# Cross-attention and ternary feed-forward: the probabilities of both tiles in five blocks of 128 keys, with new instruction orders

## The reference

```python
# layernorm(x), then attention over the 77 context rows: 16 query heads in 4 groups, 4 key heads of 32
qh = rope(layernorm(x) @ Wq); kh = rope(ctx @ Wk); vh = ctx @ Wv
scores = einsum('bghsd,bhad->bhsa', qh, kh)          # summed over the 4 groups g
attn = softmax(scores / HEAD_DIM ** 0.5, axis=-1)    # over 77 keys a
out = einsum('bhsa,bhad->bhsd', attn, vh).mean(axis=1) @ Wo
x = x + out
# feed-forward: ternary weights, input quantised to 8 bits by one scale for all of x
x = x + quantised_matmul(layernorm(x), sign(w) * (abs(w) > 0.5 * mean(abs(w)))) * scales + bias
```

## Time and profile before

| what | us |
|---|---|
| median of 3 runs | 1150.74 (1150.21 to 1151.82) |
| the profiled execution's own time | 1148.87 |
| its span, first to last instruction | 1147.1 |
| TensorE matmul busy | 1096.0 (96%) |
| VectorE busy | 1018.8 (89%) |
| ScalarE busy | 988.1 (86%) |
| GpSimd busy | 738.6 (64%), all of it before 835 us |
| mean granted TensorE clock | 0.980 of full speed |

### The profile page before, as it was taken

How to read it: one execution, slowest core, us unless ns; L and a number is a source line. 1 busy time by engine, 2 the same in 40 slices (tenths; PEclk the granted TensorE clock), 3 DMA queues, 4 the chain that set the end, 5 groups by cost and what they waited for, 6 DMA issues and landing times.

```text
span 1147.1 us, 45345 instructions
## 1 busy us (share of the span) xinstructions
PE 1096.0 (96%) x14519; PEld 894.0 (78%) x14519; DVE 1018.8 (89%) x1836; ACT 988.1 (86%) x2403; POOL 738.6 (64%) x1547
## 2 busy tenths in 40 slices
PE   7998999999999999999999999999689999999991
PEld 6997999999999999999999999999545555555550
DVE  4653799999999999999999999999889999999991
ACT  4565899999999999999999999999789999999990
POOL 4675999999999999999999999999700000000000
PEclk9999999999999999999999999999889999999996
DMA  8774365665656565665656543332029999999996
GB/s 297 217 200 132 92 218 179 203 190 193 208 188 207 177 206 181 199 200 187 212 179 208 178 147 100 98 100 79 3 111 388 423 422 427 425 418 389 401 414 281
DMA packets 97241, 260.28 MB, mean 227 GB/s; under 512 B 42537, under 2 KB 53993, under 8 KB 76722
## 3 DMA queue, kind: packets, MB, share of 16 engines
q1 hardware_dynamic: 97154, 259.75, 64.9%
q10 hardware_dynamic: 48, 0.07, 0.0%
HBM read 137.11 MB, written 122.64 MB: 226 GB/s over the span
## 4 chain that ended last, share of the span: by engine, by line
POOL 44%; PE 34%; issue 15%; DVE 2%; POOLq 1%; ACT 1%; DMA 0%; SPq 0%; DVEq 0%; ACTq 0%
PE sc_ps L1317 10%; PE pT_ps L1317 10%; POOL qr_sb L589 8%; POOL rs_sb L581 7%; POOL pw_sb L596 6%; POOL qa_sb L561 6%; PE y_ps L1112 5%; POOL pw_sb L603 5%; POOL os_sb L608 3%; POOL o_sb L610 3%; POOL ve_sb L574 2%; POOL mean L616 2%; PE xT_ps L1101 1%; PE y_ps L1300 1%; POOL os_sb L614 1%
## 5 line engine op out<-in xcount | busy, mean ns | idle before, releaser
L1257 PEld LDWEIGHTS xT_ps<-wqs,xT_sb 128*128 128x128 f32 x2048 | 239.5, 192 | 48.8 <-ACT xT_sb L723 48.8
L1257 PE MATMUL xT_ps<-wqs,xT_sb 128*128 128x128 f32 x2048 | 264.0, 282 | 2.9 <-ACT xT_sb L723 2.9
L1273 PE MATMUL pT_ps<-v_blk,pT_sb 128*128 128x68 f32 x1536 | 186.7, 271 | 0.4 <-ACT pT_sb L735 0.4
L1273 PEld LDWEIGHTS pT_ps<-v_blk,pT_sb 128*128 128x128 f32 x1536 | 182.2, 192 | 1.9 <-ACT pT_sb L735 1.2
L745 ACT ACTIVATE e_sb<-e_sb,rs_sb 128x308 f32<-128x308 f32 x256 | 127.4, 545 | 62.9 <-DVE e_sb L956 62.9
L973 DVE SCALAR_TENSOR_TENSOR x_sb<-x_sb,mv_sb,y_ps 128x512 f32 (+1 forms) x256 | 177.9, 736 | 2.7 <-PE y_ps L1249 2.7
L788 ACT ACTIVATE x_sb<-x_sb,mean 128x512 f32 (+1 forms) x256 | 168.7, 707 | 0.0
L686 ACT ACTIVATE sq_sb<-x_sb 128x512 bf16 (+1 forms) x256 | 162.6, 635 | 1.1 <-DVE x_sb L973 0.8
L980 DVE TENSOR_REDUCE amax<-x_sb (+1 forms) x128 | 155.1, 1212 | 0.0
L943 DVE TENSOR_REDUCE mx_sb<-sc_ps 128x8 f32<-128x616 f32 x128 | 102.4, 800 | 46.0 <-PE sc_ps L1238 46.0
L723 ACT ACTIVATE xT_sb<-xT_ps 128x512 f32<-128x512 f32 x256 | 139.2, 597 | 2.8 <-PE xT_ps L1179 2.7
(11 more groups left out here) (140 smaller groups left out, 2253.0 us busy)
## 6 DMA issues: line engine op xcount, KB each, us to landing
out_y<-x_sb SPq DMA_DIRECT2D x112, 1024.0 KB, 10.5
x_sb<-in_x SPq DMA_DIRECT2D x128, 512.0 KB, 3.8
x_sb<-out_y SPq DMA_DIRECT2D x48, 1024.0 KB, 15.3
x_sb<-in_ctx SPq DMA_DIRECT2D x38, 256.0 KB, 3.9
k_blk<-k_scr SPq DMA_DIRECT2D x256, 9.6 KB, 1.7
v_scr<-x_sb SPq DMA_DIRECT2D x38, 68.0 KB, 2.9
k_scr<-x_sb SPq DMA_DIRECT2D x38, 64.0 KB, 3.0
v_blk<-v_scr SPq DMA_DIRECT2D x128, 10.2 KB
```

What stands on the lines that cost most here:

```text
L1257: last = pe.matmul(bank[0][:, t * HD:(t + 1) * HD], xT_sb[:, t, c, :], wqs[:, c, :], start=c == 0, stop=c == EC - 1)
L1273: last = pe.matmul(bank[6][:, at0:at0 + 2 * VC], pT_sb[:, t, c * P:(c + 1) * P], v_blk[:, slot, c, c:c + 2, :].rearrange("p h d -> p (h d) ...
```

## The change

The probabilities of both tiles of a pair are treated as one row of 616 keys, cut in 5 blocks of 128 (starts 0, 128, 256, 384, 488). A block can reach from tile 0 into tile 1; it holds keys of 2 or 3 (tile, head) pairs, and its matmul writes all of their columns at once: 5 value matmuls of 3, 3, 2, 3, 3 x 34 columns in place of 6 of 2 x 34. `v_blk` now holds the values of a batch twice, once for each tile's place. ScalarE copies `xT_sb` and `pT_sb` with one instruction each, and both squares stand before the exponentials. GpSimd runs `pw_sb` before `qr_sb`, `o_sb` before the high part, and the mean before the low part. VectorE's `bn_stats` of tile 1 moves from the end of a step to behind the reciprocal of the next one. The diff, without the renamed semaphores and blank lines:

```diff
@@ -46,9 +46,10 @@
 HALF = P // 2
-CHUNKS = 3
-CR = -(-SC // CHUNKS)
-STARTS = [min(c * CR, SC - P) for c in range(CHUNKS)]
+CHUNKS = 5
+STARTS = [min(c * P, 2 * SC - P) for c in range(CHUNKS)]
+FIRST_HEAD, HEADS_OF = (0, 1, 3, 4, 5), (3, 3, 2, 3, 3)
@@ -91,11 +92,11 @@
 for c, start in enumerate(STARTS):
-    for h in range(HEADS):
-        lo, hi = max(c * CR, CTX * h), min(c * CR + CR, SC, CTX * (h + 1))
+    for n in range(2 * HEADS):
+        lo, hi = max(c * P, CTX * n), min(c * P + P, CTX * (n + 1))
         if lo < hi:
-            assert c <= h <= c + 1
-            out.append((c, lo - start, hi - lo, h, lo - CTX * h))
+            assert FIRST_HEAD[c] <= n < FIRST_HEAD[c] + HEADS_OF[c]
+            out.append((c, lo - start, hi - lo, n - FIRST_HEAD[c], n % HEADS, lo - CTX * n))
 return out
@@ -137,7 +138,7 @@
 e_sb = sb("e_sb", [P, 2, 2, SC])
-pT_sb = sb("pT_sb", [P, 2, CHUNKS * P])
+pT_sb = sb("pT_sb", [P, CHUNKS, P])
 pv_sb = sb("pv_sb", [P, 2, HEADS, VC])
@@ -146,7 +147,7 @@
 k_blk = sb("k_blk", [P, 2, SC])
-v_blk = sb("v_blk", [P, 2, CHUNKS, HEADS, VC])
+v_blk = sb("v_blk", [P, 2, CHUNKS, max(HEADS_OF), VC])
 bn_sb = sb("bn_sb", [P, 2, 2, 6])
...
@@ -373,8 +374,8 @@
-for c, r, n, h, a in segs:
-    sp.dma_start(v_blk[r:r + n, k % 2, c, h, :], v_scr[bass.ds(b * CTX + a, n), h, :])\
+for c, r, n, m, h, a in segs:
+    sp.dma_start(v_blk[r:r + n, k % 2, c, m, :], v_scr[bass.ds(b * CTX + a, n), h, :])\
       .then_inc(v_in[k % 2], 16)
@@ -426,7 +427,7 @@
 elif first < j <= first + 3:
-    v_step(b, b, SEGS[(j - first - 1) * 2:(j - first) * 2])
+    v_step(b, b, SEGS[(j - first - 1) * 4:(j - first) * 4])
@@ -549,24 +550,25 @@
 proj, rope, score, value, head, resid, stat, rstd = (stage(i, k, g, lag) for lag in range(RSTD + 1))
+js, ks = i - SCORE, (k - SCORE) % UN
+at = slice(0 if score else 1, 2 if rstd else 1)
+both = score or rstd
+def turned(table, dst):
+    half = slice(2 * (rope[1] % 2), 2 * (rope[1] % 2) + 2)
+    pool.tensor_tensor(dst[:, :].rearrange("p (t h d) -> p t h d", t=2, h=HEADS),
+                       q_sb[:, :].rearrange("p (t h d) -> p t h d", t=2, h=HEADS),
+                       table[:, half, :].unsqueeze(2).broadcast_to([P, 2, HEADS, D]),
+                       ALU.mult).then_inc(rope_mul, 1)
 if rope:
...
     pool.wait_ge(q_copied, j + 1)
-    half = slice(2 * (kj % 2), 2 * (kj % 2) + 2)
-    def turned(table, dst):
-        pool.tensor_tensor(dst[:, :].rearrange("p (t h d) -> p t h d", t=2, h=HEADS),
-                           q_sb[:, :].rearrange("p (t h d) -> p t h d", t=2, h=HEADS),
-                           table[:, half, :].unsqueeze(2).broadcast_to([P, 2, HEADS, D]),
-                           ALU.mult).then_inc(rope_mul, 1)
     turned(qcos, qa_sb)
-if score or rstd:
-    at = slice(0 if score else 1, 2 if rstd else 1)
-    js, ks = i - SCORE, (k - SCORE) % UN
+if both:
     if score:
@@ -575,11 +577,19 @@
     turned(qsin, qb_sb)
-if score or rstd:
+if both:
...
                        ve_sb[:, k % 2, :, at], mhalf[:, :, at], ALU.pow).then_inc(rs_ready, 1)
+if head:
+    j, kj, gj = head
+    pool.wait_ge(rinv_ready, j + 1)
+    pool.tensor_tensor(pw_sb[:, :, :, :].rearrange("p t h d -> p (t h) d"),
+                       pv_sb[:, :, :, 0:D + 1].rearrange("p t h d -> p (t h) d"),
+                       rinv_sb[:, :, :].rearrange("p t h -> p (t h)").unsqueeze(2)
+                       .broadcast_to([P, 2 * HEADS, D + 1]), ALU.mult).then_inc(o_part, 1)
 if rope:
@@ -590,14 +600,6 @@
 if head:
-    j, kj, gj = head
-    pool.wait_ge(rinv_ready, j + 1)
-    pool.tensor_tensor(pw_sb[:, :, :, :].rearrange("p t h d -> p (t h) d"),
-                       pv_sb[:, :, :, 0:D + 1].rearrange("p t h d -> p (t h) d"),
-                       rinv_sb[:, :, :].rearrange("p t h -> p (t h)").unsqueeze(2)
-                       .broadcast_to([P, 2 * HEADS, D + 1]), ALU.mult).then_inc(o_part, 1)
-if head:
     j, kj, gj = head
@@ -605,16 +607,17 @@
 pool.wait_ge(o_part, 2 * j + 2)
+pool.tensor_tensor(o_sb[:, :, :], pw2_sb[:, :, 0, :], pw2_sb[:, :, 1, :],
+                   ALU.add).then_inc(o_ready, 1)
 pool.tensor_tensor(os_sb[:, :, 0, :], pw2_sb[:, :, 0, 0:D], pw2_sb[:, :, 1, 0:D],
                    ALU.add).then_inc(o_ready, 1)
-pool.tensor_tensor(o_sb[:, :, :], pw2_sb[:, :, 0, :], pw2_sb[:, :, 1, :],
-                   ALU.add).then_inc(o_ready, 1)
+pool.wait_ge(o_ready, 2 * j + 1)
+pool.tensor_tensor(mean1[:, bass.ds(2 * j, 2)], o_sb[:, :, D], mv_sb[:, kj, :, 0],
+                   ALU.add).then_inc(mean_ready, 1)
 pool.wait_ge(o_ready, 2 * j + 2)
...
                    ALU.subtract).then_inc(os_ready, 1)
-pool.tensor_tensor(mean1[:, bass.ds(2 * j, 2)], o_sb[:, :, D], mv_sb[:, kj, :, 0],
-                   ALU.add).then_inc(mean_ready, 1)
@@ -719,23 +722,23 @@
     at_least(act, q_done, j)
-    for t in range(2):
-        act.activation(xT_sb[:, t, :, :].rearrange("p c (h r) -> p c h r", h=2),
-                       rows_of(xT_ps, t * E // 2, EC), ACT.Copy).then_inc(xT_copied_t, 1)
+    act.activation(xT_sb[:, :, :, :].rearrange("p t c (h r) -> p (t c) h r", h=2),
+                   rows_of(xT_ps, 0, 2 * EC), ACT.Copy).then_inc(xT_copied, 1)
     if isinstance(j, int) and j == 0:
         keys_out(CT, CLAST)
+if stat:
+    square(0)
 if value:
...
     at_least(act, pv_done, j)
-    for t in range(2):
-        act.activation(pT_sb[:, t, :].rearrange("p (c h r) -> p c h r", c=CHUNKS, h=2),
-                       rows_of(pT_ps, t * CHUNKS * HALF, CHUNKS), ACT.Copy).then_inc(pT_copied_t, 1)
+    act.activation(pT_sb[:, :, :].rearrange("p c (h r) -> p c h r", h=2),
+                   rows_of(pT_ps, 0, CHUNKS), ACT.Copy).then_inc(pT_copied, 1)
 if stat:
-    square(0)
+    square(1)
 if score:
@@ -751,8 +754,6 @@
     act.activation(q_sb[:, :], bank[0][:, 0:2 * HD], ACT.Copy).then_inc(q_copied, 1)
-if stat:
-    square(1)
@@ -931,6 +932,10 @@
     dve.reciprocal(rinv_sb[:, :, :], pv_sb[:, :, :, D + 1]).then_inc(rinv_ready, 1)
+if rope:
+    j, kj, gj = rope
+    dve.bn_stats(bn_sb[:, kj % 2, 1, :], x_sb[:, kj // 2, 2 * (kj % 2) + 1, :]).then_inc(bn_step, 1)
 if score:
@@ -980,10 +985,6 @@
                       apply_absolute_value=True).then_inc(amax_done, 1)
-if proj:
-    j, kj, gj = proj
-    dve.bn_stats(bn_sb[:, kj % 2, 1, :], x_sb[:, kj // 2, 2 * (kj % 2) + 1, :]).then_inc(bn_step, 1)
@@ -1218,9 +1219,9 @@
 held(exp_done_t, 2 * j + 2, exp_count, 2)
-for t in range(2):
-    for c, start in enumerate(STARTS):
-        last = halves(pT_ps, (t * CHUNKS + c) * HALF, e_sb[:, kj % 2, t, start:start + P])
+both = e_sb[:, kj % 2, :, :].rearrange("p t s -> p (t s)")
+for c, start in enumerate(STARTS):
+    last = halves(pT_ps, c * HALF, both[:, start:start + P])
 last.then_inc(pT_done, 1)
...
@@ -1264,15 +1265,14 @@
             pe.wait_ge(v_in[slot], gj * (2 * V_DMAS * 16) + (kj // 4 + 1) * (V_DMAS * 16))
-        pe.wait_ge(pT_copied_t, 2 * j + 2)
-        for t in range(2):
-            for c in (0, 2, 1):
-                at0 = (t * HEADS + c) * VC
-                last = pe.matmul(bank[6][:, at0:at0 + 2 * VC], pT_sb[:, t, c * P:(c + 1) * P],
-                                 v_blk[:, slot, c, c:c + 2, :].rearrange("p h d -> p (h d)"),
-                                 start=c == 0, stop=c == 1)
+        pe.wait_ge(pT_copied, j + 1)
+        for c in (0, 2, 4, 1, 3):
+            at0, n = FIRST_HEAD[c] * VC, HEADS_OF[c]
+            last = pe.matmul(bank[6][:, at0:at0 + n * VC], pT_sb[:, c, :],
+                             v_blk[:, slot, c, 0:n, :].rearrange("p h d -> p (h d)"),
+                             start=c == 0, stop=c == 3)
         last.then_inc(pv_done, 1)
 steps(pe, step)
```

More of the change, by code:

```diff
@@ L265, in build @@
         rs_ready = sem("rs_ready")
-        xT_done, xT_copied_t, q_done, q_copied = (
-            sem(n) for n in ("xT_done", "xT_copied_t", "q_done", "q_copied"))
+        xT_done, xT_copied, q_done, q_copied = (
+            sem(n) for n in ("xT_done", "xT_copied", "q_done", "q_copied"))
         rope_mul, qr_ready, qT_done, qT_copied = (
@@ L271, in build @@
             sem(n) for n in ("sc_done", "mx_ready", "sub_done", "exp_done_t"))
-        pT_done, pT_copied_t, pv_done, pv_copied = (
-            sem(n) for n in ("pT_done", "pT_copied_t", "pv_done", "pv_copied"))
+        pT_done, pT_copied, pv_done, pv_copied = (
+            sem(n) for n in ("pT_done", "pT_copied", "pv_done", "pv_copied"))
         rinv_ready, o_part, o_ready, os_ready, wq_mean, wq_centred = (
@@ L1253, in step @@
                     j, kj, gj = proj
-                    pe.wait_ge(xT_copied_t, 2 * j + 2)
+                    pe.wait_ge(xT_copied, j + 1)
                     for t in range(2):
```

## The result

The changed kernel takes 1133.91 us (median of 4 runs, 1128.25 to 1138.45) against 1150.47 for the kernel before beside it: a ratio of 0.9855 (95% interval 0.9809 to 0.9901). A second comparison gave 1134.54 against 1150.64, 0.9861 (0.9835 to 0.9887). It is faster by 1.4%; the forecast was 1197 us and slower.

What follows compares the result with a forecast made beforehand. TensorE bounds the kernel before; SyncE's queue would bound the changed one. Issues +31.6, holds +28.8, absorbed -8.0 and remaining steps -5.8 make +46.6 us on 1148.87: 1195.5, as a median 1197 us, range 1148 to 1242.

Steps and rivals of the forecast that it cites:

- SyncE becomes the bound: SyncE's DMA queue, batches 4 to 51: slack gone, 11.8 us a batch before added holds, against 10.82 for the compute engines.
- The compute engines' 5.41 us a step: Four compute engines: a step falls from 5.59 to 5.41 us, 0.18 less, with VectorE as their bound.
- The gap before the maximum: VectorE: the moved bn_stats directly before the maximum makes it wait, adding 0.04 us a step.
- The price of six more issues, 2.88 us: SyncE's queue: 12 v pieces instead of 6, each added issue at 0.48 us, 2.88 us more a batch.
- s = 0.6: SyncE's queue: change in time of held issues per batch, taken as +0.6 us, bounds -2.5 and 2.2.
- the two rate terms: SyncE's loop: +28.7 us for 47 batches at 11.8 instead of 11.19, and +28.8 for 48 x 0.6 of holds.
- the tail: The 32 steps after SyncE's loop: run at the compute engines' pace, 0.18 us less each, -5.8 us.
- the 8.0 us of v slack: Between the last v piece's landing and its first reader: delay absorbed there, -8.0 us in the sum.
- the 2.9 of the last batch: End of SyncE's loop: the last batch's own six added issues, +2.9 us in the sum.
- Break-even: SyncE's period at which loss and gain cancel within 0.2%: 11.4 us a batch, chance 0.09.
- the first rival: SyncE does not bind: holds shrink 0.4 us a batch for break-even, 1.0 to clear it; 1129 us, chance 0.16.

Runs made afterwards that it cites:

- e1: The changed kernel with 4 of each batch's 12 v pieces left out, so part of the value product is missing: 1123.74 us, ratio 0.9767.
- g1: The changed kernel with the loop's x1 stores issued by ScalarE instead of SyncE: 1125.96 us, ratio 0.9788.
- g2: g1 with VectorE's bn_stats of tile 1 back at the end of the step: 1123.81 us, ratio 0.9770.
- h1: The changed kernel with the 12 v pieces issued ahead of the x1 store in SyncE's loop: 1124.87 us, ratio 0.9772.
- i1: g2 without the last of four feature chunks in tile 0's q projection, so its q is incomplete: 1115.98 us, ratio 0.9697.
- e3: The changed kernel with the old orders on GpSimd, ScalarE and VectorE; five blocks, 12 v pieces and single copies stay: 1147.73 us, ratio 0.9969.
- g3: The kernel before with the x1 stores issued by ScalarE: 1153.29 us, ratio 1.0023.
- f1: The kernel before with each of its 6 v pieces cut in two, 12 issues for the same rows: 1168.66 us, ratio 1.0145.
- f2: The kernel before with each of its 6 v pieces brought twice, the second time to an unread spare tile: 1155.72 us, ratio 1.0050.

## Why the prediction was wrong, point by point

**SyncE becomes the bound: right.** Its wait for x1 fell from 91.1 us to 1.1 and e1 gave it back. TensorE waits for x, as was named as one of two possibilities, not for `v_blk`.

**The compute engines' 5.41 us a step: right in size, by luck, and wrong in the engine.** 5.40 in the tail and in e1, g1, g2, h1. It is TensorE's bound (i1). Two errors met: TensorE was to take 5.27 and takes 5.40; VectorE was to take 5.41, and in its old order it runs 5.35 (i1). TensorE's matmul records had been priced by their weight loads alone. The value matmuls' weight loads fell by 12 x 0.118 - 10 x 0.120 = 0.22 us (forecast 0.24) and the transposes by 0.06 (0.08). All loads together went from 460.05 us at 5.594 a step to 454.70 at 5.397 (g1): 5.15 to 4.91 us, -0.24. The rest of TensorE's step, in which no load ran, grew from 0.45 to 0.49 us. The single copies took 1.026 and 0.697 us (1.02 and 0.70 forecast). The gap before the maximum was right: in g1 the maximum has 4.1 us of idle time in 83, 1.2 of them a wait for the scores, so 0.035 us each. GpSimd had three waits on itself; with the one before `pw2_sb` in the earlier trace rows, the other two were:

```profile
L608 POOL TENSOR_TENSOR os_sb<-pw_sb 128x64 fp32r<-128x64 f32 x80 | 24.0, 300 | 10.2
...
L614 POOL TENSOR_TENSOR os_sb<-o_sb,os_sb 128x64 fp32r<-128x64 f32 x80 | 25.3, 317 | 6.3
```

Of these 6.4, 10.2 and 6.3 us the first and the last are gone, as forecast, 0.16 us a step; the middle one stays and stands before `o_sb` now (10.5). e3 shows that the new orders were needed to get below 5.56.

**The price of six more issues, 2.88 us, with s = 0.6 us of hold on top: this step failed.** From the first v piece to the first k piece it was 4.89 us a batch and is 6.97 (means of 47 batches): +2.08, where 3.48 was forecast. The forecast took the hold for a length that comes on top of the issues. It ends at a point of time: 4.35 us behind the second x load's issue before (mean; the one batch of the earlier trace rows has 4.26), 4.90 now, +0.55, with x loads that land at 5.7 us instead of 4.1. That later end is what s = 0.6 foresaw, but it is no term of its own, as more issues fit before it. Up to the first issue behind the hold it is 3.35 us before and 3.89 now, and in it stand mostly five of the twelve pieces (27 of 47 batches; four in 12) instead of three of six. So about seven, not nine, are paid behind it: 2 x 0.48 = 1.0 us less. And these seven cost 0.44 us each, not 0.48 to 0.51, as some of them find their address ready: 0.4 us less.

The control runs give the same in the prediction's two terms. Without holds the six pieces take 3.07 us from the start of the first to the start of the issue behind them (g3, mean; 3.02 in the batch shown), the twelve 5.44 (h1, mean; 514.42 - 509.05 = 5.37 in the batch above):

```profile
502.80 2.74 SPq L377 DMA_DIRECT2D v_blk<-v_scr  x6
505.82 1.82 SPq L371 DMA_DIRECT2D k_blk<-k_scr  x4
```

That makes 2.37 us for six more issues, 0.40 each, where 2.88 was forecast. The time in holds is then 4.89 - 3.07 = 1.82 us a batch before and 6.97 - 5.44 = 1.53 now: s was -0.3, not +0.6. The rest of a batch's queue stayed at 4.0 us. The need is 8.91 + 2.08 = 11.0, and 11.00 was measured.

**The sum, made again with what was measured.** The loop starts 0.7 us earlier; 47 x (11.03 - 11.19) = -7.5 in place of the +57.5 that the two rate terms gave together; the tail 32 x (5.40 - 5.60) = -6.4 (forecast -5.8); together -14.6, and -14.8 were measured. So neither the 8.0 us of v slack nor the 2.9 of the last batch appear. The slack was read off the wrong transfer: TensorE stopped for x, whose loads fall behind with the queue from the first batches on (four waits from 140 to 200 us, up to 1.4 us each), and no wait for a v piece appears at all. With the 4.3 us lost in the second part, which lies within what that part varies by, it is -10.3, measured -10.6.

**Break-even** was put at 11.4 us a batch, with the v slack in it; it lies at the period of before, 11.19: f1's 47 x (11.54 - 11.19) = +16.5 stands against a last maximum that starts 15.4 us later (831.6) and 17.8 us by the medians. An error of 13% in the need, 12.4 for 11.0, decided the sign, as what counts is its distance from 11.2, times 47. In the prediction's unit the outcome is 11.0 - 11.8 = -0.8 us a batch, between the 0.4 and the 1.0 of the first rival, which had a chance of 0.16. That rival was right that the time in holds shrinks, by 0.3 us, and the cheaper issues gave the rest; it was wrong that SyncE then does not bind.

**The Trainium skill's sentence** (DMA: Bandwidth & Descriptors, section Issuing engines are not separate DMA queues) that the time to initiate a DMA "is usually small relative to the DMA itself" holds here of each DMA alone: a k piece's issue takes 0.32 us and it lands after 1.7. It does not follow that issues cost nothing, and the prediction was right not to go by that: 4 fewer give 10 us (e1), and 6 more cost 18 (f1). That section's subject, which sequencer issues, is what g1 used.

**What stays open** is what an issue waits for when it is held. With the store in SyncE's queue right behind the x loads, the hold stands at the second to fifth v piece; in g1, h1 and i1, where it does not stand there, shorter holds appear at the eleventh to sixteenth issue behind the x loads; in g3, with 10 small issues and no store, there is hardly any. A limit on what is in flight would fit all of it, but no run measured one.

## What to carry to other kernels

When an in-order queue that issues DMAs runs near its slack, don't price added issues one by one on top of its stalls: find the instant at which a stall ends, count how many issues fit before it and pay only for those behind. When a forecast rests on the difference of two nearly equal periods, the sign is settled by an error of a few per cent, so the chance must be split near even however clear the bound is. And when a queue is the bound, first look for the order of its own entries: small transfers that others wait for belong ahead of a large store that nobody waits for (1134 to 1125 us here for an exchange of two lines).

## What the runs showed of the hardware that was not expected

- With the 1 MB store in front of them, small DMA issues of SyncE are held, two a batch in the kernel before and two to four in the changed one, until 4.35 and 4.90 us on average behind the second x load's issue; without it in front, the first nine pieces take 0.23 to 0.35 us each (g1; so do all six in g3, but for one issue in 47 batches), and the holds come later or hardly at all.
- An issue with an address computed in registers starts 0.18 to 0.2 us after its forerunner's end, 0.09 if the address is already there (f2, alternating). Over 12 issues that and the hold make 0.32 us a batch (11.54 against 11.22).
- The x loads land later when both are issued close together with the store right behind: median 5.7 us in the changed kernel and f1 (loads 0.7 us apart), 4.8 in e1 (1.9 apart), 4.1 in the kernel before (2.9 apart). Without the store behind them it is 4.0 in g1 (1.4 apart) and 4.4 in h1 (1.1 apart, the store behind the v pieces). No run changes the distance or the store alone.
